# Writing out the loops of projection and attention, and moving a batch's output products into the next unit

## What is computed

```python
Q = (x @ WQ + bQ).reshape(b, s, h, dh).transpose(0, 2, 1, 3)   # K, V alike
scores = jnp.einsum('bhqd,bhkd->bhqk', Q, K) / scale
scores = jnp.where(causal, scores, jnp.float32(-100000.0))
A = jax.nn.softmax(scores, axis=-1)
Z = jnp.einsum('bhqk,bhkd->bhqd', A, V)
out = jnp.einsum('bhsd,de->bse', Z, WO) + jnp.float32(h) * bO
...
x = x + 0.5 * _L0_ffn_ref(_layernorm(x, axis=-1), ...)
x = x + _L0_attn_ref(_layernorm(x, axis=-1), ...)
x = x + 0.5 * _L0_ffn_ref(_layernorm(x, axis=-1), ...)
```

## Time and profile before

| | us |
|---|---|
| median of 3 runs | 1563.81 (1563.08 to 1564.3) |
| profiled execution | 1566.32 |
| its span, first to last instruction | 1564.6 |
| first feed-forward layer, to about | 455 |
| projection, to about | 560 |
| attention, to about | 1125 |
| second feed-forward layer, to about | 1565 |

### The profile page before, as it was taken

The page is one execution under the profiler, slowest core; times in us unless marked ns, Lnnn a source line. Parts: engine busy times, 40 slices in busy tenths (PEclk is TensorE's granted clock), DMA queues, the critical chain, the costliest instruction groups (busy, mean ns, idle before and its releaser), DMA issues. The chain is left out here.

```text
span 1564.6 us, 32677 instructions
## 1 busy us (share of the span) xinstructions
PE 1416.8 (91%) x9796; PEld 964.5 (62%) x9796; DVE 1033.0 (66%) x2636; ACT 775.6 (50%) x1317; POOL 640.7 (41%) x679
## 2 busy tenths in 40 slices
PE   4899999999978869999999899999698999999997
PEld 3687888888856623343333333333276878888886
DVE  5575646366788678887788688786267564445567
ACT  4312566555135424665566466567451245655530
POOL 3361443767645460232222122223235406176765
PEclk9899999999989957999999899999789999999999
DMA  7651566888326910443335253300131227588873
GB/s 256 223 201 57 179 199 193 263 249 249 99 74 163 237 66 1 65 61 43 43 43 67 34 67 43 42 3 2 41 107 63 94 71 230 159 254 248 261 235 109
DMA packets 159221, 199.08 MB, mean 127 GB/s; under 512 B 18180, under 2 KB 132440, under 8 KB 159064
## 3 DMA queue, kind: packets, MB, share of 16 engines
q1 hardware_dynamic: 140632, 146.67, 36.0%
q0 software_dynamic: 18432, 50.36, 10.1%
HBM read 105.21 MB, written 91.49 MB: 126 GB/s over the span
## 5 line engine op out<-in xcount | busy, mean ns | idle before, releaser
L1636 ACT ACTIVATE attn_prob<-attn_b_ps 128x1024 f32<-128x1024 f32 (+3 forms) x352 | 303.8, 870 | 214.9 <-PE attn_b_ps L1838 213.8
L505 POOL DMA_INDIRECT xs_dram<-ffn_xn,ffn_index x192 | 188.4, 981 | 228.8 <-DVE ffn_index L780 172.5
L1818 PE MATMUL attn_a_ps<-k_rows,q_rows 96*128 96x512 bf16 (+3 forms) x768 | 252.3, 352 | 24.5 <-DVEq L1674 7.5
L519 POOL DMA_INDIRECT ffn_gathered<-ys_dram,ffn_index x192 | 196.6, 1024 | 86.8 <-issue 56.1
L1687 DVE TENSOR_REDUCE attn_max_a<-attn_a_ps 128x1 f32<-128x512 f32 (+2 forms) x304 | 202.6, 688 | 43.3 <-PE attn_a_ps L1818 24.1
L1573 POOL TENSOR_SCALAR_AFFINE_SELECT attn_prob<-attn_prob 128x512 f32<-128x512 f32 x128 | 81.1, 634 | 359.2 <-ACT attn_prob L1636 356.6
L824 DVE TENSOR_TENSOR ffn_xs_lo<-ffn_xt_ps,ffn_xs_hi 128x512 fp32r<-128x512 f32 x144 | 97.7, 678 | 154.8 <-ACT ffn_xs_hi L596 154.3
L1818 PEld LDWEIGHTS attn_a_ps<-k_rows,q_rows 96*128 96x128 bf16 x768 | 75.3, 99 | 189.9 <-DVE attn_max_a L1687 79.9
L1862 PE MATMUL attn_o_ps<-attn_prob,attn_v_now 128*17 128x256 f32 (+1 forms) x2560 | 189.0, 368 | 0.0
L1838 PE MATMUL attn_b_ps<-q_rows,k_rows 98*128 98x512 bf16 (+3 forms) x768 | 187.9, 333 | 0.3 <-ACT attn_prob L1636 0.3
L1684 DVE CUSTOM_DVE_ANT_0 attn_scored<-attn_a_ps,mask_wide 128x512 bf16<-128x512 f32 (+1 forms) x256 | 155.1, 623 | 40.2 <-PE attn_a_ps L1818 35.3
(11 more groups left out here) (209 smaller groups left out, 2732.2 us busy)
## 6 DMA issues: line engine op xcount, KB each, us to landing
ffn_xs<-xs_dram SPq DMA_DIRECT2D x138, 256.0 KB, 3.5
ys_dram<-ffn_y SPq DMA_DIRECT2D x138, 256.0 KB, 2.9
xs_dram<-ffn_y SPq DMA_DIRECT2D x16, 768.0 KB, 11.2
qk_parts<-proj_cut SPq DMA_DIRECT2D x32, 384.0 KB, 3.0
k_rows<-qk_parts SPq DMA_DIRECT2D x96, 128.0 KB, 4.7
q_rows<-qk_parts SPq DMA_DIRECT2D x96, 128.0 KB, 7.4
ffn_w_stage<-in_L_ffn_w_dram SPq DMA_DIRECT2D x64, 128.0 KB, 2.5
x_res<-in_L_attn_x_dram SPq DMA_DIRECT2D x4, 1024.0 KB, 8.7
```

The lines of the kernel that those rows point to most:

```text
L505: pool.indirect_dma_start(xs_dram[(b + 1) % 2], bass.IndirectOffsetOnAxis(index[:, b, i, k:k + 1], 0), xn[:, b % 2, i, :], None, bounds_ch ...
L519: pool.indirect_dma_start(gathered[:, t % G_RING, k, :], None, ys_dram[b], bass.IndirectOffsetOnAxis(index[:, b, i, k:k + 1], 0), bounds_c ...
L1636: act.activation(prob[PROB[kt]][:, h:h + heads, prob_at(kt, kt * P):prob_at(kt, S)], b_ps[:, slot, :].rearrange("p (h t) -> p h t", h=head ...
L1818: ins = pe.matmul(a_ps[:, bank, i * keys:end], q_rows[q][0:SROWS, h0 + i, qt * P:(qt + 1) * P], k_rows[q][0:SROWS, h0 + i, first:first + k ...
```

## The change

All `Fori` loops of `project` and `attention` become Python loops, so that the program of each engine is straight-line code, with numbers in place of registers. `Ring` and `Steps` lose the base that counted loop turns.

`output` and `add_output` now do one pair at a call. For the last batch both pairs stay behind step 11 of its last quad. For the three others the first pair moves behind step 13 and the second behind step 15 of the first quad of the next batch (`OUTPUT_LATER`). The transposes of z stay behind step 10.

```diff
             for c in range(first, first + QUADS):
                 store(c, c - first)
-            with sp.Fori(first + QUADS, CHUNKS) as c:
+            for c in range(first + QUADS, CHUNKS):
                 store(c)
...
-            with act.Fori(0, CHUNKS - 1) as c:
+            for c in range(0, CHUNKS - 1):
                 take(c, (c + 1) % 2, True)
...
-            with pool.Fori(0, CHUNKS - 2) as c:
+            for c in range(0, CHUNKS - 2):
                 norm.ready.pool_root(pool, c + 2)
...
-            with dve.Fori(0, CHUNKS - 2) as c:
-                steps.base = c * per
+            for c in range(0, CHUNKS - 2):
                 chunk(c, (c + 1) % 2, True, True)
-                assert steps.n == at + per
...
-            with pe.Fori(0, CHUNKS // 2 - 1) as pair:
+            for pair in range(0, CHUNKS // 2 - 1):
                 for par in range(2):
...
-        a_first = len(banks) + early + 1 + sum(beside_n[:LEAD])
-        a_seq = QUADS * (len(banks) + 1) + 2 + QT // 2
-        assert a_seq % 2 == 0
+        OUTPUT_LATER = (13, 15)
...
             def __init__(self):
-                self.base, self.n, self.odd = 0, 0, 0
+                self.n = 0
 
             def take(self):
-                bank, number = (self.odd + self.n) % 2, self.base + self.n
                 self.n += 1
-                return bank, number
-
-            def sequence(self, b):
-                self.base, self.n, self.odd = a_first + b * a_seq, 0, a_first % 2
+                return (self.n - 1) % 2, self.n - 1
 
...
-            with sp.Fori(0, B - 1) as b:
+            for b in range(0, B - 1):
                 sequence(b, False)
...
-            with act.Fori(0, B - 1) as b:
+            for b in range(0, B - 1):
...
-            def add_output(b):
-                for i in range(QT // 2):
+            def add_output(b, pair):
+                for i in (2 * pair, 2 * pair + 1):
                     bank, number = ring.take()
                     dve.wait_ge(a_ready, number + 1)
...
             def sequence(b, last):
-                ring.sequence(b)
                 for q in range(QUADS):
                     more = not last or q < QUADS - 1
                     more2 = not last or q < QUADS - 2
                     for n in range(LEAD, steps_n):
                         step(q, n, more, more2)
+                        if b and q == 0 and n in OUTPUT_LATER:
+                            add_output(b - 1, OUTPUT_LATER.index(n))
...
                             take_z()
-                        if q == QUADS - 1 and n == OUTPUT_AT + 1:
-                            add_output(b)
+                        if last and q == QUADS - 1 and n == OUTPUT_AT + 1:
+                            add_output(b, 0)
+                            add_output(b, 1)
 
             at = steps.n
             per = QUADS
-            with dve.Fori(0, B - 1) as b:
-                steps.base = b * per
+            for b in range(0, B - 1):
                 sequence(b, False)
-                assert steps.n - at == per, (steps.n - at, per)
-            steps.base = (B - 2) * per
             sequence(B - 1, True)
 
...
-            def output(b):
+            def output(b, pair):
                 pe.wait_ge(z_turned, b + 2)
-                for pair in range(0, QT // 2, 2):
-                    places = [(j, *ring.take()) for j in (pair, pair + 1)]
+                places = [(j, *ring.take()) for j in (2 * pair, 2 * pair + 1)]
+                for j, bank, number in places:
+                    pe.wait_ge(a_free, number + 1)
+                for half in range(2):
                     for j, bank, number in places:
-                        pe.wait_ge(a_free, number + 1)
-                    for half in range(2):
-                        for j, bank, number in places:
-                            ins = pe.matmul(a_ps[:, bank, half * D:(half + 1) * D], z_t[32 * j:32 * j + 32, half, :],
-                                            wo_rows[32 * j:32 * j + 32, :], start=True, stop=True,
-                                            tile_position=(32 * j, 0))
-                            if half == 1:
-                                ins.then_inc(a_ready, 1)
+                        ins = pe.matmul(a_ps[:, bank, half * D:(half + 1) * D], z_t[32 * j:32 * j + 32, half, :],
+                                        wo_rows[32 * j:32 * j + 32, :], start=True, stop=True,
+                                        tile_position=(32 * j, 0))
+                        if half == 1:
+                            ins.then_inc(a_ready, 1)
...
             def sequence(b, last):
-                ring.sequence(b)
                 for q in range(QUADS):
                     more = not last or q < QUADS - 1
                     more2 = not last or q < QUADS - 2
                     for n in range(LEAD, steps_n):
                         step(b, q, n, more, more2)
+                        if b and q == 0 and n in OUTPUT_LATER:
+                            output(b - 1, OUTPUT_LATER.index(n))
                     for n in range(LEAD):
                         if more:
                             step(b + (q + 1) // QUADS, (q + 1) % QUADS, n, more2, None)
...
                             turn_values(b, q, more)
                         if q == QUADS - 1 and n == OUTPUT_AT:
                             turn_z(b)
-                        if q == QUADS - 1 and n == OUTPUT_AT + 1:
-                            output(b)
-
-            with pe.Fori(0, B - 1) as b:
+                        if last and q == QUADS - 1 and n == OUTPUT_AT + 1:
+                            output(b, 0)
+                            output(b, 1)
+
+            for b in range(0, B - 1):
                 sequence(b, False)
             sequence(B - 1, True)
```

More of the change, by code:

```diff
@@ L1608, in _ @@
             per = 2 + 3 * (QUADS - 2) + 2
-            with pool.Fori(0, B - 1) as b:
-                steps.base = b * per
+            for b in range(0, B - 1):
                 sequence(b, False)
-                assert steps.n - at == per, (steps.n - at, per)
-            steps.base = (B - 2) * per
             sequence(B - 1, True)
@@ L1690, in join_maxima @@
             def join_maxima(q):
-                dve.wait_ge(a_free, ring.base + ring.n + 2)
+                dve.wait_ge(a_free, ring.n + 2)
                 dve.tensor_tensor(max_a[:, q % 2, :, QT // 2:], max_a[:, q % 2, :, QT // 2:], max_b[:, q % 2, :, :],
```

## The result

The changed kernel takes 1557.51 us, the kernel before 1563.03 us, both medians of 20 runs beside each other. The ratio is 0.9965, with a 95% interval of 0.9952 to 0.9977: 5.5 us faster (3.6 to 7.5), where 12.7 were forecast. The three runs of before that the prediction started from lay close together by chance. In the 20, but for one execution of 2251.27 us that the ratio leaves out, the kernel before goes from 1557.75 us up to 1568.4, and the changed one from 1550.37 to 1563.2.

What follows compares the result with a forecast made beforehand. TensorE was taken to set attention's pace, with 29.38 us lost at three batch changes. Gains of 3.60 (jump), 8.68 (clock) and 0.45 (products) summed to 12.73 us, from 1563.81 to 1551.1 us; whole range 1547.8 to 1560.0.

Steps and rivals of the forecast that it cites:

- The jump: Attention's loop edge on TensorE at the first two changes of batch: 1.70 and 1.90 us, 3.60 us gained by writing loops out.
- The products moved: Output products behind steps 13 and 15 still cost TensorE 2.50 and 2.31 us, 14.43 in three batches against 14.88 before.
- Straight-line code: In a regular attention unit, written-out code was to cost TensorE nothing against loops: both units took 30.76 us.
- The clock: TensorE's granted clock after the output products was to stay at 2.4 GHz, giving back 8.68 us over three batches.
- The sum: Three changes of batch take 108.93 us in place of 121.66, a gain of 12.73 us.
- The projection: This stage waits for transfers, so its written-out loops gain zero; at most 0.8 us gained or 1.70 lost.
- the second: Rival: the low clock stays in all three batches, 1561.3 us at full price or 1559.8 at today's; chance 0.10.
- the first rival: The low clock stays in one or two batches, 3.41 us each, giving 1554.5 to 1557.9 us; chance 0.22.
- the likeliest case: The forecast itself: clock at 2.4 GHz throughout the changes of batch, 1551.1 us; chance 0.58.

## Why the prediction was half right

Its own steps, one by one:

- **The jump** (3.60 us). Right, by step 11: 6.11 us with the loops alone, 7.96 to 8.40 where a jump follows, 6.18 to 6.30 where none does. No branch is left on TensorE in attention. The kernel with the loops alone has all three distances at 39 us, as the one change without a jump had in rows 3; in the two later profiles of before that one takes 37.9, with a low stretch half as long. The Trainium skill states the reason that fits: "Runtime: NRT & Kernel Launch", section "Instruction fetch mechanics", says that a taken branch to code that is not at hand waits for a fetch. Rows 6 agree, with 3.43 and 3.64 us taken against 0.083 not taken; no run here shows the fetch itself.
- **The products moved** (14.43 us in three batches). Right, almost to the number: 2.44 + 2.34 = 4.78 a batch, 14.34 in three, and 36.28 us instead of 36.31 for a whole change of batch where the clock stays up. The waits that the prediction built from rows 4, 5 and 8 are where it put them.
- **Straight-line code** costs no more than loops in a unit. Right: 30.76 us.
- **The clock** (8.68 us). This is the step that failed, in two ways. First its size: it was read from one execution. Jump and clock together were 3.60 + 8.68 = 12.28 us there. In the two later profiles of before, less the same 2.22 us of z and 14.88 of products, they are 26.5 - 17.1 = 9.4 and 25.6 - 17.1 = 8.5; the mean of three is 10.05. Second, the value chosen for after: the clock was taken to stay up, with 0.58, and fell in two or three batches of each profile, 11 of 15 in all. The mean excess after is 19.95 us; less 2.22 of z and 14.34 of products, 3.4 us of low clock are left.
- **The sum**, redone with these: 10.05 - 3.39 + 0.54 of products = 7.2 us instead of 12.73, which is also the difference of the mean excesses, 27.15 - 19.95. Of the 5.5 us that are missing, 2.2 were not there to win in the mean of three, and 3.4 stayed with the clock (the products gave 0.1 more than forecast).
- **The projection** (0 taken, 0.8 at most). Mis-sized in the other direction: 104.5 us before and 103.4 after in the mean of three and five profiles, and 2 us over all kernels. The loads begin about 0.7 us earlier, counted from the stage's first product; of that, 0.2 lies between the first store and the first load. The rest was not followed up.
- **What was not in the sum**: a low stretch in the last batch, 1.6 us in three of five profiles after and in none of three before. The wait of 1.17 us ahead of it stands at the same place in all fourteen profiles, those of before too. The stretch comes and goes between executions of one program and was seen in four other kernels of the study, but those have the moved products as well, and none of the four profiles with the products at their old place has it. Whether the change makes it likelier stays open.

Added up, the profiles give 7.2 + 1.1 - 1.0 = 7.3 us, and the runs 5.5 (3.6 to 7.5). They agree within the interval, at its upper end. The remaining difference lies inside the spread of the other stages and was not traced further; the mean granted clock is 0.958 in the 20 runs of after and 0.960 in the five profiles, so the runs may hold somewhat more low clock than the profiles show.

Of the rivals, the first came true in four profiles of five, and the second in the profile after itself, where the clock fell in all three batches. The low clock stayed, at 1.55 instead of 3.41 us a time, since a stretch of 3.41 us took the place of one of 6.82. That the time, 1557.5, lies where the first rival ends (1557.9) is in part luck: the falls cost half its price, and 2.2 us of what was to be won were not there. What spoke for it was in the prediction, that the stops do not vanish. The argument against it, that they are shorter and have steps between them, was too weak: one pair with its two stops, 0.60 and 0.75 us, was enough in the kernel with the projection's loops. The rule of the Trainium skill that was weighed there ("TensorE: Matmul & The Clock Gate", section "A second HAM failure mode: psum-queue depth-cycling"), on brief idling between groups of matmuls, came nearer than the forecast: the clock fell in 11 of 15 batches, not in all. The filled kernel shows that the idling takes part in it, as filling most of the stop ahead of each pair keeps the clock up. The time lies within the stated range, but the likeliest case was the wrong one.

## What to carry to other kernels

Moving work into a busy stretch did not hide it here, where two engines share a ring of two buffers: count the waits that the new place brings, as the old place's waits come along. Then look at what the waits do to the clock before pricing them by their length alone, and read such a term from several executions, as it differs between executions of one program. Here the fastest kernel gave TensorE other work of its own inside the wait, and set the pairs far apart: 1548.0 us, 0.8% below the kernel before. Filling a stop with useless work came to 1549.8 us, which the intervals don't tell from it.

## What the runs showed of the hardware that was not expected

- Behind a pair of products of 1.13 us with stops of 0.32 and 0.83 us around it, the clock fell to 1.2 GHz in 11 of 15 changes of batch, and twice in another kernel behind the first pair, with stops of 0.60 and 0.75 us. With two matmuls of 0.2 us each in the stop ahead of each pair it stayed at 2.4 GHz in all three batches of the profile.
- The four matmuls of one place hold TensorE for 1.06 us, the eight of a pair for 1.07 (737.34 - 736.27). The pair's start two by two, within 0.04 us of each other, so its two row groups run side by side, and splitting a pair doubles its cost on TensorE.
- The low stretches at the changes of batch are 3.41, 6.83 or 10.24 us long in these profiles, and begin at another point of the work in each execution. In three profiles of the kernel before, the excess at these changes goes from 25.6 to 29.4 us with them.
